# A stack of four graph layers on one core: two of four low parts moved from GpSimd to VectorE, and the hand-written order of all four engines changed

## The chip, the cores and the metric

The kernel runs on one core of a Trainium2 chip. The metric is the device time in microseconds (us) of one execution. The kernel before takes 1517.57 us, the median of 3 runs (1515.54 to 1517.81).

## What is computed

128 graphs of 128 nodes with 256 features pass through four layers. Each layer normalises its input over the features, applies ReLU, works on the result and adds it back. Cut to what matters (matrices per graph, `H` is 1 where the adjacency is not 0):

```python
# layer 1: hypergraph convolutions; Dn, Be are inverse degrees
h  = relu(Dn * (H @ (Be * (H.T @ (x @ W1.T)))) + b1)      # 512 features
h  = layer_norm(h, gamma, beta)
y  = Dn * (H @ (Be * (H.T @ (h @ W2.T)))) + b2 + x
# layer 2: attention with leaky ReLU, masked at 0.5, softmax over the nodes, ELU
h  = elu(softmax(where(adj > 0.5, leaky(Wh1 + Wh2.T), NEG_INF), axis=1) @ (x @ W))
# layer 3: diffusion, T = A * exp(leaky(...)), rows normalised
h  = relu(x @ Wk0 + bk0 + (T @ x) @ Wk1 + bk1 + (T @ (T @ x)) @ Wk2 + bk2)
# layer 4: one weight per node from masked scores, softmax over the nodes
h  = softmax(sum((q @ k.T) / 8 * adj, -1), axis=nodes) * (x @ Wv.T)
```

## The kernel before

**Tiling.** The graphs are taken in 32 groups of four (`G = 4`). A tile is [128 nodes, 4 graphs, features]. The products with a weight matrix run in a split form: an operand is written as a high part in the type fp32r plus a low part, the rest that the high part leaves, and TensorE adds three passes, high times high, high times low and low times high (`split_product`, L321 for the first two passes and L325 for the last one). Products without a split run in plain fp32 (`product`, L306), transposes too (`transposes`, L434). The high part of an activation is a copy by ScalarE out of PSUM; the low part is a subtraction by VectorE or GpSimd.

**Stages.** A round works on five groups at once: `next` (group i+1: counts, degrees, norm of the input), `front` (group i: layer 1 and the attention of layer 2), `mid` (group i-1: the ELU and layer 3), `late` (group i-2: layer 4) and `tail` (group i-3: the softmax over nodes and the output). Rounds 0 to 3 and 31 to 34 are written out with what they have; rounds 4 to 30 are one loop (`rounds`, `steady=True`).

**Order.** Nothing but the text sets the order: each engine has a function `body(r)` that calls its blocks one after the other, and each block first waits on semaphores (`wait_ge`). An engine takes its blocks in that order and no other, so a block that waits holds back everything behind it on its engine. PSUM has eight banks, and many waits are for a bank to be read out.

**The blocks around the change.** On TensorE `front_w1(r, 0..3)` makes the hidden layer (512 features x 512 nodes in four parts), `mid_h2` transposes `h` of layer 3, which VectorE's `mid_ln2` wrote, and `front_w2(r, g)` multiplies the hidden layer with W2. The first wait of `front_w2(r, 0)` is for PSUM bank 3, in which ScalarE's `tail_exp` reads the row of the tail group. `mid_p1`, `mid_p2` and `mid_p0` are the three products of layer 3, all out of the transposes. `tail_row` and `tail_turn` turn the tail group's weights there and back. ScalarE's `copy_u` (L744) writes each part of the hidden layer twice, `hT` in fp32 and `hT_hi` in fp32r, and `copy_h2T` (L754) writes the high part of the transposes. The low parts of the hidden layer are `front_lo(r, 0..3)` on GpSimd (L961), an fp32 subtraction of two SBUF tiles, 128x512; in round 0 alone VectorE makes the third and the fourth (`first_low`, L1116). TensorE's last pass of `front_w2` waits until all four are there:

```python
wait(pe, S["wex_ready"], r.tail(G))        # front_w2, g = 0 and 1
pe.wait_ge(S["hT_hi"], r.front(G))
split_product(..., 0, (S["hT_lo"], r.front(G))).then_inc(S["zr_ready"], 1)
```

GpSimd also adds the hidden layer up for its variance (`add_h` L975, `add_squares` L966, `join_h` L979, `join_squares` L971; TensorE's `front_sums` needs both results), computes every `rsqrt` as a power of -0.5 (L954 and L956), and does the elementwise sums `add_res0`, `mask_edges`, `add_xb`, `add_x4`, `add_bias` and `add_x3`. VectorE's `mid_low` (L1120) makes the low part of the transposes out of PSUM, `mid_columns` (L1301) waits for `rs2_ready`, which GpSimd's `rsqrt(2, ...)` gives. In round 0 GpSimd's `wide_lows` (L1042) makes the low parts of the weights of layers 3 and 4.

**Queues.** SyncE issues all loads and stores; no engine of the four issues a DMA. In every round it loads the adjacency and the input of the next group, stores the output and copies one adjacency tile.

## Time and profile before

| what | us |
|---|---|
| median of 3 runs | 1517.57 |
| the profiled execution, its own time | 1514.74 |
| the span of its instructions | 1512.9 |
| TensorE matmuls busy | 1461.8 (97%) |
| TensorE weight loads busy | 1321.6 (87%) |
| VectorE busy | 1230.0 (81%) |
| GpSimd busy | 1067.9 (71%) |
| ScalarE busy | 945.4 (62%) |

The granted TensorE clock is 0.99 over the span. The profile was taken from an execution of its own, so its durations are held against its own time, 1514.74 us. In the rows PE is TensorE, DVE VectorE, ACT ScalarE, POOL GpSimd; L is the line of the kernel. Matmuls are pipelined and their ends are modelled, so that a row of TensorE that looks full can hold short waits; the starts show them.

### The profile page before, as it was taken

How to read it: one execution, taken by the hardware profiler on the slowest of the kernel's cores; microseconds unless marked ns; L12 is line 12 of the kernel's file. 1: busy time of each engine (PE TensorE's matmuls, PEld its weight loads, DVE VectorE, ACT ScalarE, POOL GpSimd, SP SyncE). 2: the span in 40 equal slices, each digit the busy share in tenths (PEclk: the TensorE clock that was granted, in tenths of full speed). 3: DMA queues.
4: the chain of work that ended last, by engine and by line, in shares of the span. 5: the costliest groups of instructions: out<-in, count | busy, mean ns of one | idle time of the engine just before them, and what ended most of it. 6: DMA issues, size and time to landing. Idle time of an engine off the chain costs nothing.

```text
span 1512.9 us, 35521 instructions
## 1 busy us (share of the span) xinstructions
PE 1461.8 (97%) x9944; PEld 1321.6 (87%) x9944; DVE 1230.0 (81%) x4491; ACT 945.4 (62%) x2122; POOL 1067.9 (71%) x1070
## 2 busy tenths in 40 slices
PE   7889999999999999999999999999999999999975
PEld 5779998989998988998988998988998988998964
DVE  6779888889888889888889888889888889888773
ACT  4556666766666766666766666766566766566744
POOL 5666787676787676787676787676787676787724
PEclk9999999999999999999999999999999999999997
DMA  3011011111011111011111011111011111011001
GB/s 126 22 36 36 16 50 35 49 49 49 16 46 35 49 49 49 21 42 35 49 49 49 21 42 35 49 49 49 21 42 35 49 49 49 22 41 35 28 29 50
DMA packets 75373, 62.05 MB, mean 41 GB/s; under 512 B 3013, under 2 KB 70985, under 8 KB 75338
## 3 DMA queue, kind: packets, MB, share of 16 engines
q1 hardware_dynamic: 75338, 61.63, 12.5%
q8 instruction: 16, 0.26, 0.1%
q14 instruction: 19, 0.16, 0.0%
HBM read 36.45 MB, written 16.78 MB: 35 GB/s over the span
## 4 chain that ended last, share of the span: by engine, by line
PE 69%; DVE 18%; issue 8%; ACT 2%; POOL 1%; DVEq 1%; DMA 0%; POOLq 0%; ACTq 0%; SPq 0%
PE ps L321 29%; PE ps L306 18%; PE ps L325 15%; PE ps L434 5%; DVE stats L1207 3%; PE ps L372 2%; DVE x L1295 2%; DVE h L1225 2%; DVE q L1374 2%; DVE wh L1402 2%; DVE el L1288 2%; DVE yT_lo L1116 1%; DVE pT L1380 1%; ACT ps L812 1%; DVE qmax L1386 1%
## 5 line engine op out<-in xcount | busy, mean ns | idle before, releaser
L722 ACT ACTIVATE p<-ps,rs 128x256 f32<-128x256 f32 x384 | 164.2, 472 | 275.4 <-PE ps L325 192.9
L1009 POOL TENSOR_TENSOR x3n<-p,x 128x512 f32<-128x512 f32 x64 | 80.9, 1285 | 257.0 <-ACT p L802 257.0
L961 POOL TENSOR_TENSOR hT_lo<-hT,hT_hi 128x512 fp32r<-128x512 f32 x126 | 162.9, 1295 | 65.3 <-ACT hT_hi L744 59.2
L956 POOL TENSOR_TENSOR rs<-var_e,neg_half 128x4 f32<-128x4 f32 x160 | 165.0, 1031 | 23.7
L321 PE MATMUL ps<-wl_hi,h2T_hi 128*128 128x256 f32 (+1 forms) x768 | 168.9, 301 | 0.0
L325 PE MATMUL ps<-wl_hi,h2T_lo 128*128 128x256 f32 (+1 forms) x768 | 154.5, 283 | 0.0
L321 PE MATMUL ps<-wl_lo,h2T_hi 128*128 128x256 f32 (+1 forms) x768 | 154.4, 282 | 0.0
L434 PE MATMUL ps<-ident,h 128*128 128x128 f32 x768 | 131.9, 283 | 11.9 <-DVE h L1225 5.9
L722 ACT ACTIVATE vqk<-ps,rs 128x384 f32<-128x384 f32 x128 | 74.1, 579 | 106.8 <-POOL rs L956 60.8
L306 PE MATMUL ps<-p,alT 128*128 128x256 f32 (+1 forms) x512 | 127.1, 380 | 0.8 <-DVE z L1346 0.8
L434 PEld LDWEIGHTS ps<-ident,h 128*128 128x128 f32 x768 | 90.4, 145 | 41.7 <-DVE h L1225 19.6
L321 PEld LDWEIGHTS ps<-wl_hi,h2T_hi 128*128 128x128 f32 x768 | 120.9, 190 | 2.4 <-issue 0.2
L321 PEld LDWEIGHTS ps<-wl_lo,h2T_hi 128*128 128x128 f32 x768 | 118.4, 189 | 0.0
L325 PEld LDWEIGHTS ps<-wl_hi,h2T_lo 128*128 128x128 f32 x768 | 118.0, 189 | 0.0
L1225 DVE TENSOR_SCALAR_CACHE_REDUCE h<-x,mv 128x256 f32<-128x256 f32 x256 | 113.6, 463 | 2.3
L1207 DVE BATCH_NORM_STATS2 stats<-x 128x6 f32<-128x256 f32 x256 | 108.6, 424 | 4.5
L306 PEld LDWEIGHTS ps<-p,alT 128*128 128x128 f32 x512 | 89.7, 189 | 14.3 <-issue 1.6
L744 ACT ACTIVATE hT<-ps,cols_sb 128x512 f32<-128x512 f32 x128 | 87.8, 686 | 9.9 <-PE ps L325 8.0
L1301 DVE TENSOR_TENSOR sij<-ps,rs 128x8 f32<-128x8 f32 x32 | 5.3, 167 | 108.4 <-POOL rs L956 105.0
L1020 POOL TENSOR_TENSOR p<-p,bk 128x512 f32<-128x512 f32 x64 | 82.7, 1292 | 13.1 <-ACT p L722 12.2
L744 ACT ACTIVATE hT_hi<-ps,cols_sb 128x512 fp32r<-128x512 f32 x128 | 87.6, 684 | 3.5
L321 PE MATMUL ps<-w_hi,hT_hi 128*128 128x256 f32 x512 | 88.3, 295 | 1.1
(176 smaller groups left out, 4565.2 us busy)
## 6 DMA issues: line engine op xcount, KB each, us to landing
x_in<-in_x SPq DMA_DIRECT2D x32, 512.0 KB, 4.5
out_x<-x SPq DMA_DIRECT2D x32, 512.0 KB, 2.9
adj_f<-in_adjT SPq DMA_DIRECT2D x32, 256.0 KB, 3.6
adj_m<-in_adjT SPq DMA_DIRECT2D x32, 256.0 KB, 2.8
adj_l<-adj_m SPq DMA_DIRECT2D x32, 256.0 KB, 2.3
vqk<-in_l_wk SPq DMA_DIRECT2D x3, 256.0 KB, 4.7
x<-in_w2T SPq DMA_DIRECT2D x1, 512.0 KB, 6.6
x<-in_w1T SPq DMA_DIRECT2D x1, 512.0 KB, 7.5
```

Source lines behind the costliest of these rows:

```text
L306: last = pe.matmul(dst, lhsT(c), rhs(c), start=(c == 0), stop=(c == chunks - 1))
L321: pe.matmul(dst, lhsT(a, c), rhs(b, c), start=(a == b == c == 0), stop=False)
L325: last = pe.matmul(dst, lhsT(1 - late, c), rhs(late, c), start=False, stop=(c == chunks - 1))
L434: last = pe.transpose(ps[:, banks[b], ((g % 2) * KC + c) * P:((g % 2) * KC + c + 1) * P], h[:, g, c * P:(c + 1) * P], ident[:])
L722: return act.activation(dst, src, ACT.Copy, scale=scale)
L744: act.activation(dst[:, hc, :], ps[:, U_BANKS[hc], :], ACT.Relu, bias=cols_sb[:, 0, hc:hc + 1]).then_inc(S[ready], 1)
L956: pool.tensor_tensor(rs[:, layer, :], var_e[:, layer, :], neg_half[:], ALU.pow).then_inc(done, G)
L961: pool.tensor_tensor(hTs[1][:, hc, :], hT[:, hc, :], hTs[0][:, hc, :], ALU.subtract).then_inc(S["hT_lo"], 1)
L1009: pool.tensor_tensor(x3n[:, s], p0[:, s], x2[:, s], ALU.add).then_inc(S["x3_ready"], 2)
L1020: pool.tensor_tensor(p0[:, s, :], p0[:, s, :], bk[:].rearrange("p (a d) -> p a d", a=1) .broadcast_to((P, 2, D)), ALU.add).then_inc(S["p0b ...
L1207: dve.bn_stats(stats[:, layer, g, :], src[:, g, :]).then_inc(st, 1)
L1225: dve.tensor_scalar(dst[:, g, :], src[:, g, :], mv[:, layer, g, 0:1], None, ALU.subtract, ALU.add, accum_out=unread[:, layer, g:g + 1]).th ...
```

## The change

GpSimd no longer makes the low parts 2 and 3 of the hidden layer; VectorE does, in every round (`hidden_low`, the old `first_low` under a new name), and on all four engines blocks stand in another order. In `gnn_stack` nothing else differs: no instruction is added or left out but that two subtractions change their engine, and no buffer, bank or wait is changed. The diff, with twelve leading blanks of each line left out:

```diff
@@ -606,47 +606,49 @@
     if r.has_front:
         front_w1(r, 0)
         front_w1(r, 1)
+        front_w1(r, 2)
+        front_w1(r, 3)
     if r.has_tail:
         tail_row(r)
-    if r.has_front:
-        front_w1(r, 2)
-        front_w1(r, 3)
     if r.has_mid:
         mid_h2(r, 0)
         mid_h2(r, 1)
+        mid_p1(r, 0)
+        mid_p1(r, 1)
     if not r.steady and r.i == 0:
         second_rows(r)
         first_weights(r)
     if r.has_front:
         front_w2(r, 0)
     if r.has_mid:
-        mid_p1(r, 0)
+        mid_p2(r, 0)
     if r.has_tail:
         tail_turn(r)
     if r.has_mid:
-        mid_p2(r, 0)
         mid_p2(r, 1)
         mid_p2(r, 2)
         mid_p2(r, 3)
     if r.has_front:
         front_w2(r, 1)
     if r.has_mid:
-        mid_p1(r, 1)
         mid_b2(r)
-    if r.has_front:
-        front_w2(r, 2)
-    if r.has_mid:
         mid_p1(r, 2)
+    if r.has_front:
+        front_sums(r, 0)
+    if r.has_mid:
         mid_p1(r, 3)
+    if r.has_front:
+        front_sums(r, 1)
     if r.has_late:
         late_h3(r, 0)
     if r.has_front:
-        front_sums(r, 0)
-        front_sums(r, 1)
         front_sums(r, 2)
-        front_sums(r, 3)
     if r.has_late:
         late_h3(r, 1)
+    if r.has_front:
+        front_sums(r, 3)
+        front_w2(r, 2)
+    if r.has_late:
         late_vqk(r, 0)
     if r.has_front:
         front_w2(r, 3)
@@ -655,31 +657,32 @@
         mid_ap(r, 1)
         mid_ap(r, 2)
         mid_ap(r, 3)
+    if r.has_late:
+        late_vqk(r, 1)
     if r.has_front:
         front_c2(r, 0)
         front_c2(r, 1)
+    if r.has_mid:
+        mid_az(r, 0)
+    if r.has_front:
         front_c2(r, 2)
-    if r.has_late:
-        late_vqk(r, 1)
+    if r.has_mid:
+        mid_az(r, 1)
     if r.has_front:
         front_c2(r, 3)
     if r.has_mid:
-        mid_az(r, 0)
-        mid_az(r, 1)
         mid_p0(r, 0)
         mid_p0(r, 1)
     if r.has_next:
         next_s(r, 0)
+        next_s(r, 1)
     if r.has_mid:
         mid_p0(r, 2)
-    if r.has_next:
-        next_s(r, 1)
+        mid_az(r, 2)
+    if r.has_front:
+        front_h1(r, 0)
     if r.has_mid:
         mid_p0(r, 3)
-    if r.has_front:
-        front_h1(r, 0)
-    if r.has_mid:
-        mid_az(r, 2)
         mid_az(r, 3)
     if r.has_front:
         front_h1(r, 1)
@@ -839,35 +842,36 @@
         copy_u(r, 1)
         copy_u(r, 2)
         copy_u(r, 3)
+    if r.has_mid:
+        copy_h2T(r, 0)
+    if r.has_front:
+        square(r, 0)
     if r.has_tail:
         tail_exp(r)
     if r.has_mid:
-        copy_h2T(r, 0)
         copy_h2T(r, 1)
     if r.has_front:
-        square(r, 0)
         square(r, 1)
     if r.has_tail:
         weigh(r, 0)
+    if r.has_mid:
+        copy_p1(r, 0)
     if not r.steady and r.i == 0:
         wide_hi()
     if r.has_mid:
         copy_p2(r, 0)
         copy_p2(r, 1)
-        copy_p1(r, 0)
         exp_edges(r, 0)
         exp_edges(r, 1)
         copy_p1(r, 1)
+        copy_p2(r, 2)
     if r.has_late:
         copy_h3T(r, 0)
-    if r.has_mid:
-        copy_p2(r, 2)
-    if r.has_late:
         copy_h3T(r, 1)
+    if r.has_mid:
+        copy_p2(r, 3)
     if r.has_tail:
         weigh(r, 1)
-    if r.has_mid:
-        copy_p2(r, 3)
     if r.has_late:
         copy_vqk(r, 0, 6)
     if r.has_mid:
@@ -876,6 +880,7 @@
         copy_s(r, 0)
     if r.has_late:
         copy_vqk(r, 1, 7)
+        keep_x3(r)
     if r.has_next:
         copy_s(r, 1)
     if r.has_front:
@@ -886,9 +891,6 @@
         copy_h1T(r, 1)
     if r.has_next:
         norm_x(r, 0)
-    if r.has_late:
-        keep_x3(r)
-    if r.has_next:
         norm_x(r, 1)
     if r.has_late:
         copy_vqk(r, 2, 2)
@@ -896,10 +898,10 @@
         softmax(r, 0)
     if r.has_late:
         copy_vqk(r, 3, 3)
+    if r.has_front:
+        softmax(r, 1)
     if r.has_next:
         copy_yT(r, 0)
-    if r.has_front:
-        softmax(r, 1)
     if r.has_mid:
         relu_p0(r)
     if r.has_next:
@@ -1054,48 +1056,48 @@
 def body(r):
     if r.has_front:
         front_lo(r, 0)
+        add_h(r, 0)
         front_lo(r, 1)
-    if r.has_front and (r.steady or r.i > 0):
-        front_lo(r, 2)
-        front_lo(r, 3)
-    if r.has_front:
-        add_h(r, 0)
+    if r.has_mid:
+        rsqrt(2, mv[:, 2, :, 1], S["ag2"], r.mid(G), S["var2"], S["rs2_ready"])
+    if r.has_front:
+        add_h(r, 1)
         add_squares(r, 0)
-        add_h(r, 1)
-    if r.has_mid:
-        rsqrt(2, mv[:, 2, :, 1], S["ag2"], r.mid(G), S["var2"], S["rs2_ready"])
-    if r.has_front:
         add_squares(r, 1)
         join_h(r)
         join_squares(r)
         add_res0(r, 0)
-        add_res0(r, 1)
     if r.has_mid:
         mask_edges(r)
-    if r.has_front:
-        rsqrt(4, hmean[:, 1, :], S["hvar_ready"], r.front(G), S["vare_h"], S["rsh_ready"])
     if not r.steady and r.i == 0:
         wide_lows()
     if r.has_late:
         rsqrt(3, mv[:, 3, :, 1], S["ag3"], r.late(G), S["var3"], S["rs3_ready"])
+    if r.has_front:
+        rsqrt(4, hmean[:, 1, :], S["hvar_ready"], r.front(G), S["vare_h"], S["rsh_ready"])
+    if r.has_next:
+        rsqrt(0, mv[:, 0, :, 1], S["ag0"], r.next(G), S["var0"], S["rs0_ready"])
+    if r.has_tail:
+        add_x4(r, 0)
+    if r.has_front:
+        add_res0(r, 1)
     if r.has_next:
         add_xb(r, 0)
     if r.has_tail:
-        add_x4(r, 0)
-    if r.has_next:
-        rsqrt(0, mv[:, 0, :, 1], S["ag0"], r.next(G), S["var0"], S["rs0_ready"])
+        add_x4(r, 1)
+    if r.has_mid:
+        add_bias(r, 0)
+    if r.has_front:
+        rsqrt(1, mv[:, 1, :, 1], S["ag1"], r.front(G), S["var1"], S["rs1_ready"])
+    if r.has_mid:
+        add_bias(r, 1)
+    if r.has_next:
         shift_x(r)
-        add_xb(r, 1)
-    if r.has_tail:
-        add_x4(r, 1)
-    if r.has_mid:
-        add_bias(r, 0)
-    if r.has_front:
-        rsqrt(1, mv[:, 1, :, 1], S["ag1"], r.front(G), S["var1"], S["rs1_ready"])
-    if r.has_mid:
-        add_bias(r, 1)
+    if r.has_mid:
         add_x3(r, 0)
         add_x3(r, 1)
+    if r.has_next:
+        add_xb(r, 1)
 
 def first(r):
     rsqrt(0, mv[:, 0, :, 1], S["ag0"], r.next(G), S["var0"], S["rs0_ready"])
@@ -1191,7 +1193,7 @@
     dve.wait_ge(S["cols_ready"], 4)
     dve.memset(c0[:, 4:5], 0.0).then_inc(S["cols_ready"], 1)
 
-def first_low(r, hc):
+def hidden_low(r, hc):
     dve.wait_ge(S["hT_hi"], r.front(hc + 1))
     dve.wait_ge(S["hT_ready"], r.front(hc + 1))
     low(hTs, (slice(None), hc), hT[:, hc, :]).then_inc(S["hT_lo"], 1)
@@ -1457,8 +1459,6 @@
 
 def body(r):
     if not r.steady and r.i == 0:
-        first_low(r, 2)
-        first_low(r, 3)
         first_dots()
     if r.has_mid:
         elu_low(r, 0)
@@ -1472,40 +1472,42 @@
     if r.has_mid:
         elu_high(r, 0)
         elu_high(r, 1)
+        mid_ln2(r)
     if r.has_tail:
         tail_max(r)
     if r.has_mid:
-        mid_ln2(r)
+        mid_low(r, 0)
+    if r.has_front:
+        hidden_low(r, 2)
+        hidden_low(r, 3)
+    if r.has_tail:
+        tail_norm(r)
+    if r.has_mid:
+        mid_low(r, 1)
     if r.has_next:
         next_count(r)
     if r.has_tail:
-        tail_norm(r)
-    if r.has_mid:
-        mid_low(r, 0)
-    if r.has_next:
-        next_inverse(r)
-    if r.has_mid:
-        mid_low(r, 1)
-    if r.has_tail:
         tail_out(r)
+    if r.has_next:
+        next_moments(r)
     if r.has_mid:
         mid_columns(r)
     if r.has_late:
         late_ln3(r)
-    if r.has_next:
-        next_moments(r)
     if r.has_mid:
         mid_edges(r)
+    if r.has_next:
+        next_inverse(r)
     if r.has_late:
         late_low(r, 0)
     if not r.steady and r.i == 0:
         second_dots()
     if r.has_front:
         front_variance(r)
+    if r.has_next:
+        next_binc(r)
     if r.has_late:
         late_low(r, 1)
-    if r.has_next:
-        next_binc(r)
     if r.has_front:
         front_z(r, 0)
         front_z(r, 1)
@@ -1523,9 +1525,11 @@
         degree_masked(r)
     if r.has_front:
         front_low(r, 0)
+    if r.has_mid:
+        mid_vb(r, 0)
+    if r.has_front:
         front_low(r, 1)
     if r.has_mid:
-        mid_vb(r, 0)
         mid_vb(r, 1)
     if r.has_front:
         front_columns(r)
@@ -1536,18 +1540,17 @@
         front_logits(r, 1)
         front_leaky(r, 0)
         front_max(r, 0)
+    if r.has_next:
+        next_penalty(r)
+    if r.has_front:
         front_leaky(r, 1)
-    if r.has_next:
-        next_penalty(r)
-    if r.has_front:
         front_max(r, 1)
         front_inverse(r, 0)
         front_values(r, 0)
-    if r.has_next:
-        y_low(r.next(2), 0)
-    if r.has_front:
         front_inverse(r, 1)
         front_values(r, 1)
+    if r.has_next:
+        y_low(r.next(2), 0)
 
 def first(r):
     next_count(r)
```

## Rows read from the trace of the kernel before

**Rows 1.** The page, busy time of the engines.

```profile
PE 1461.8 (97%) x9944; PEld 1321.6 (87%) x9944; DVE 1230.0 (81%) x4491; ACT 945.4 (62%) x2122; POOL 1067.9 (71%) x1070
```

**Rows 2.** Waits in 190 to 1412 us (who waited: us in total, times, longest).

```profile
PEld ps L321 <- ACT wex L749: 7.5, 27, 0.3
DVE sij L1301 <- POOL rs L956: 89.0, 27, 3.3
```

**Rows 3.** The chain that ended last, 725.7 to 741 us (start, us, what).

```profile
739.45 0.48 DVE h L1225 x3
```

**Rows 4.** Timeline of TensorE in a steady round (start, us, what, [idle before]).

```profile
739.24 1.80 PE L434 MATMUL ps<-ident,h 128*128 128x128 f32 x8
741.08 0.74 PE L321 MATMUL ps<-w_hi,hT_hi 128*128 128x256 f32 x4
741.66 0.62 PE L321 MATMUL ps<-w_lo,hT_hi 128*128 128x256 f32 x4
742.19 0.74 PE L325 MATMUL ps<-w_hi,hT_lo 128*128 128x256 f32 x4
742.77 0.40 PE L321 MATMUL ps<-wl_hi,h2T_hi 128*128 128x256 f32 x2
```

**Rows 5.** Timeline of VectorE in the same round.

```profile
735.41 1.28 DVE L1295 SCALAR_TENSOR_TENSOR x<-ps,el 128x512 f32<-128x512 f32 x2
736.75 0.28 DVE L1417 TENSOR_REDUCE wsm<-ps 4x1 f32<-4x128 f32 x1
736.96 0.41 DVE L1207 BATCH_NORM_STATS2 stats<-x 128x6 f32<-128x256 f32 x1
...
740.47 0.28 DVE L1234 TENSOR_SCALAR_CACHE_REDUCE inc_T<-adj_f 128x128 f32<-128x128 f32 x1
...
741.36 0.14 DVE L1439 RECIPROCAL wsm<-wsm 4x1 f32<-4x1 f32 x1
...
741.91 0.67 DVE L1120 SCALAR_TENSOR_TENSOR h2T_lo<-ps,h2T_hi 128x512 fp32r<-128x512 f32 x1
```

**Rows 6.** Timeline of ScalarE in the same round.

```profile
738.07 0.69 ACT L744 ACTIVATE hT<-ps,cols_sb 128x512 f32<-128x512 f32 x1 [0.22 <-PE ps L325]
...
740.02 0.68 ACT L744 ACTIVATE hT<-ps,cols_sb 128x512 f32<-128x512 f32 x1
...
740.93 1.05 ACT L754 ACTIVATE h2T_hi<-ps 128x512 fp32r<-128x512 f32 x2
```

**Rows 7.** Timeline of GpSimd in the same round.

```profile
736.56 2.66 POOL L961 TENSOR_TENSOR hT_lo<-hT,hT_hi 128x512 fp32r<-128x512 f32 x2 [1.39 <-ACT hT_hi L744]
...
745.83 0.26 POOL L954 TENSOR_SCALAR var_e<-mv 128x4 f32<-128x4 f32 x1
746.24 1.03 POOL L956 TENSOR_TENSOR rs<-var_e,neg_half 128x4 f32<-128x4 f32 x1
```

**Rows 8.** Timeline of the start, VectorE and GpSimd: two-tile subtractions that overlap.

```profile
20.03 1.22 DVE L1149 TENSOR_TENSOR w_lo<-x,w_hi 128x1024 fp32r<-128x1024 f32 x1
20.48 1.93 POOL L961 TENSOR_TENSOR hT_lo<-hT,hT_hi 128x512 fp32r<-128x512 f32 x1 [1.53 <-ACT hT_hi L744]
23.61 1.72 POOL L975 TENSOR_TENSOR hsq<-hT 128x512 f32<-128x512 f32 x1
24.62 1.26 DVE L1116 TENSOR_TENSOR hT_lo<-hT,hT_hi 128x512 fp32r<-128x512 f32 x1 [0.42 <-ACT hT L744]
```

**Rows 9.** Timeline of the start: GpSimd's power and VectorE's scalings inside it.

```profile
8.34 1.10 POOL L956 TENSOR_TENSOR rs<-var_e,neg_half 128x4 f32<-128x4 f32 x1
9.04 0.88 DVE L1132 TENSOR_SCALAR x<-x,cols_sb 128x256 f32<-128x256 f32 x3 [0.22 <-DMA x<-in_w2T]
```

**Rows 10.** Timelines of rounds 0 and 1, GpSimd and TensorE.

```profile
36.34 0.25 POOL L954 TENSOR_SCALAR var_e<-hmean 128x4 f32<-128x4 f32 x1 [1.88 <-DVE hmean L1338]
37.76 3.46 POOL L1042 TENSOR_TENSOR wl_lo<-vqk,wl_hi 128x512 fp32r<-128x512 f32 x3
...
80.57 0.67 PE L306 MATMUL ps<-p,alT 128*128 128x257 f32 x2 [0.77 <-DVE z L1346]
```

18 lines of the change are left out of this document (9 added, 9 removed).

## The prediction, made before the changed kernel had run

> **What bounds the kernel now.** I read the page first: TensorE's matmuls are busy 97% of the span, VectorE 81%, GpSimd 71% [rows 1]. Then the waits of the loop's stretch: what stands there 27 times stands there once a round, so a round is 1222 / 27 = 45.26 us [rows 2]. Four rounds written out, 27 in the loop and four to drain make up the rest.
>
> A TensorE that is 97% busy would leave only the number of matmuls to save, and the change saves none. So I read the chain that ended last and the timelines. In every round the chain leaves TensorE after the transposes of the degrees (about 726 us in the round shown), runs through VectorE, the softmax, the ELU and the norm of layer 3 up to the last `h` [rows 3], and comes back to TensorE when the eight transposes of `h` can end: eight of them take 1.80 us there [rows 4], where they would take about 0.9 at TensorE's pace of 0.11 us each, which I take from the four matmuls of 128x256 that start within 0.45 to 0.58 us [rows 4]. So a round is one loop of two pieces: about 15 us of VectorE, and 30 us of TensorE in which it has no real slack. What shortens the round is a wait inside the TensorE piece or an instruction inside the VectorE piece. What ends on GpSimd or ScalarE counts only where one of the two waits for it.
>
> In the TensorE piece I see two waits right behind the transposes. `front_w2(r, 0)` waits for ScalarE's `tail_exp`: 7.5 us in 27 rounds, 0.28 us each [rows 2]. Its last pass then waits for GpSimd's fourth low part: the starts 741.66, 742.19 and 742.77 are 0.53 and 0.58 us apart where four such matmuls at full pace take 0.46 (741.66 is itself a pass at full pace), so 0.07 of wait and 0.12 of restart, 0.19 in all [rows 4]. GpSimd is late in another place too: VectorE's `mid_columns` waits 3.3 us a round for `rs2` [rows 2], but the products `mid_p2` that it also needs end only shortly before, so this wait costs nearly nothing.
>
> **The change, part by part, per steady round.**
>
> *TensorE after the transposes.* `mid_p1(0)` and `mid_p1(1)` now come first, then `front_w2(0)`. The wait for `tail_exp` goes: the two products stand before it (0.7 us each: three passes at about 0.24 from the start at 742.77 on), minus 0.28. The wait for the fourth low part goes as well, minus 0.19. New is that `mid_p1(0)` has no cover between the transposes and their copy. The first half of the transposes is ready near 740.0; ScalarE is free after its last `hT` copy, which now comes as before or a little earlier, 740.0 to 740.1 + the copy of 0.57 [rows 6], so the high part is there at 740.7, as TensorE arrives: no wait. VectorE's `mid_low(0)` starts when the copy ends and its end is 0.67 later [rows 5], 741.45, where TensorE wants it at about 741.3 (two high passes and 0.11 for the start): 0.1 to 0.2 of wait and a restart of 0.11, plus 0.3.
>
> *VectorE, the two low parts.* No instruction of a steady round is a subtraction of two SBUF tiles by VectorE. A VectorE operation of 128x512 that reads PSUM takes 0.68 and starts its follower 0.60 later (two `elu_high` in 1.28) [rows 5]; alone I take the same, 2 x 0.60 = 1.2 us. They stand between `mid_low(0)` and `tail_norm`, in the 3.3 us in which VectorE waits for `rs2` [rows 2], so they cost nothing by themselves; but `mid_low(1)` stands behind them and `mid_p2(0)` waits for it. Times: `mid_low(0)` 740.8, the two low parts 741.4 and 742.0, `tail_norm` 742.6 to 743.15 (0.55 from its first start to the next block [rows 5]), `mid_low(1)` up to 743.8. TensorE has two `mid_p1` and one `front_w2` (1.5) behind the wait above and comes to `mid_p2(0)` at about 743.9. Cost 0 to 0.1, and I take 0.05.
>
> *VectorE's piece of the loop.* `tail_max` leaves it: between the end of `elu_high` at 736.69 and the norm's first start at 736.96 lie 0.27 us [rows 5]; without it a gap of 0.06, as in front of 736.75, is left: minus 0.2. `next_penalty` now stands ahead of the second `front_leaky` instead of between it and its `front_max`, so a gap of such a size opens: plus 0.07. Sum minus 0.13.
>
> *GpSimd.* Two subtractions of about 1.3 [rows 7] go, 2.6 us a round. `rs2` comes some 4 us earlier, and `mask_edges`, `rs4` and `join_squares` earlier too. Nothing in the steady loop waits for these now but `mid_columns`, so I count 0. `shift_x` and the second `add_xb` move to the end: `shift_x` ends about 1 us before VectorE's part for the attention needs ScalarE again, and `norm_x` fits in ScalarE's idle time there. 0.
>
> *The other moves* (`mid_az` between `front_c2`, `front_sums` between `mid_p1` and `late_h3`, `next_moments` into VectorE's idle time, `mid_vb(0)` between the `front_low`, `softmax(1)` ahead of a copy) keep the matmuls of TensorE's piece the same set. `front_att` ends 0.4 us earlier, but this lies beside VectorE's piece: 0. `mid_az(0)` waits for `mid_z1(0)`, which needs all four `mid_ap`; `late_vqk(1)` and two `front_c2` cover it. No queue of SyncE is passed.
>
> Sum of a steady round: -0.28 - 0.19 + 0.3 + 0.05 - 0.13 = -0.25 us; the bounds are -0.5 (no new wait) and +0.1 (both new waits twice as long). Over 28 rounds: -7 us, bounds -14 and +3.
>
> *The start.* In round 0 `wide_lows` now stands ahead of `rsqrt(4)`. Three of its four operations take 3.46, the fourth has 768 columns instead of 512, about 1.7: 5.2 us; against this GpSimd had waited 1.88 for the variance [rows 10], and one `add_res0` (1.3) moves behind: z comes 2.0 us later, plus 2.0. In round 1 TensorE waits 0.77 for z [rows 10] and more for GpSimd before it, since the whole round hangs on GpSimd there; 2.6 us less of it give about -1.2, round 2 about -0.5. Sum +0.3. In the drain `tail_max` stands in the norm's way once: -0.3.
>
> Sum: 1514.74 - 7 + 0 = 1507.7 for the profiled execution, minus 7 (0.5%). The median shown is 2.8 above that execution, so 1517.57 - 7 = 1510.5.
>
> **The lock between VectorE and GpSimd.** In the start two-tile operations of both overlap. GpSimd's subtraction at 20.48 began inside VectorE's of 20.03 to 21.25 and took 1.93 instead of 1.3; VectorE's at 24.62 began inside GpSimd's addition of 23.61 to 25.33 and took 1.26 instead of 0.68 [rows 8]. So the later one stands still until the earlier one is done, or nearly. Where do the new subtractions fall? GpSimd in the steady round: third `hT` copied at 738.3 (ScalarE, 738.07 before, some 0.4 earlier now) [rows 6], `add_h(0)`, `front_lo(1)` of 1.25 each, 0.4 for the add of epsilon, the power of 1.03 [rows 7]: the power runs 741.2 to 742.25, then `add_h(1)`. The subtractions run 741.4 to 742.6: beside the power. That power took 1.10 at 8.34 to 9.44, and VectorE's three scalings started inside it at their own pace, 0.88 for three [rows 9]; so a power does not hold VectorE, and I count 0. Only GpSimd's `add_h(1)` is put off by 0.4, and `join_squares` still ends 0.5 us before `front_sums`.
> The Trainium skill (SBUF — State Buffer, "SBUF: two separate sides") says that the shared pair of ports is an exclusive lock which the operation that starts first holds for the whole instruction, for a VectorE operation with two SBUF inputs against a GpSimd one that reads SBUF. The trace agrees on the elementwise ones [rows 8]; on the power no row here has a two-input VectorE operation. By that rule the time would be that of the third rival.
>
> **The rivals.**
> 1. *The new waits eat it.* If `mid_p1(0)` waits 0.4 for copy and low part and `mid_p2(0)` 0.2, the round stays within 0.1 of 45.26: 1514 to 1520. For it speaks that every margin above is under 0.2 us. Chance 0.19.
> 2. *The second low part meets `add_h(1)`.* The margin is 0.25 us (742.0 against 742.25). If VectorE is later by that, it stands still for 1.25, `mid_low(1)` ends at 745.2, and `mid_p2(0)` waits 1.3 more: a round of -0.25 + 1.3 = +1.05, over 28 rounds +29: 1547; met in a part of the rounds, or with part of the wait covered, 1521 to 1547. It decides once VectorE comes to the second low part over 0.25 us later than above. Against it: both engines start from the same ScalarE copies. Chance 0.15.
> 3. *The power holds the lock.* The first low part, started 0.2 after the power, stands still 0.85, and the second then falls behind `add_h(1)`: 0.85 + 1.25 = 2.1 a round minus 0.25 and 0.05 of margin, +1.8, over 28 rounds +50: 1567. The scalings in [rows 9] speak against it. Chance 0.06.
> 4. *The forecast*, a round of 44.75 to 45.15: 1503 to 1514. Chance 0.6.
>
> **How the numbers follow.** A measurement of this kernel can tell about 0.2% (3 us) from no change. Faster by more: 0.6, the forecast. Within: 0.18, most of the first rival. Slower: 0.22, rivals 2 and 3 and the rest of the first. The range takes the forecast with its bounds and the first rival and part of the second: 1502 to 1526; outside are the full rivals 2 and 3 and a small chance below.
>
> **What would show it.** In the profile after: no row of `PEld ps L321 <- ACT wex`; TensorE's `ps<-wl_hi,h2T_hi` directly behind the transposes, its `h2T_lo` pass 0.1 to 0.3 late; the steady round 45.0; VectorE's `hT_lo` rows at about 0.68, beside GpSimd's power, and not at 1.2 or more; VectorE's wait for `rs` gone; GpSimd's `wl_lo` ahead of `rs` in round 0 and z 2 us later. Wrong I would be if the `hT_lo` rows are stretched, if `mid_p2(0)` waits for `h2T_lo` by more than 0.3, or if a steady round is 45.2 or longer.

## The result, and the profile after

The changed kernel took 1531.71 us (median of 4 runs, 1531.37 to 1533.54) against 1517.69 (4 runs, 1515.54 to 1519.71) of the kernel before: the ratio is 1.010, with a 95% interval of 1.0087 to 1.0113. It is slower by 1%, where I had forecast 1510.5 and a range up to 1526. The profiled execution took 1531.81 with a span of 1530.0, 17.1 us longer than the span of before. The medians are 14.0 apart: the profiled execution of before, 1514.74, lies 3 us under its median, that of after on it, so some 3 of the 17 belong to the two executions and not to the kernels.

Where the 17 us of the profiles lie can be read from the start of the first `w1` matmul of each round. Each column is the time between two such starts (rounds 4 to 31: the mean of 27), in us:

| | round 0 | rounds 1 to 3 | a round, 4 to 31 | last stretch |
|---|---|---|---|---|
| before | 39.50 | 133.14 | 45.27 | 100.54 |
| after | 42.96 | 133.34 | 45.70 | 102.49 |
| loss | +3.5 | +0.2 | +0.43 x 27 = +11.6 | +1.9 |

The last stretch begins with round 31, which still has its front part. If that round lost 0.43 as the others did, the drain itself lost 1.5.

The page, busy time of the engines, against [rows 1]:

```profile
PE 1471.3 (96%) x9944; PEld 1330.9 (87%) x9944; DVE 1279.2 (84%) x4553; ACT 938.1 (61%) x2122; POOL 1006.8 (66%) x1008
```

The move is plainly there: VectorE does 62 instructions and 49 us more, GpSimd 62 fewer and 61 us less.

The waits of the steady rounds, 193 to 1427 us, against [rows 2] (who waited: us in total, times, longest):

```profile
PEld ps L325 <- DVE yT_lo L1118: 9.2, 27, 0.3
DVE h2T_lo L1122 <- ACT h2T_hi L757: 8.5, 27, 0.3
...
DVE sij L1303 <- PE ps L325: 6.3, 26, 0.2
...
PEld ps L325 <- DVE h2T_lo L1122: 5.3, 27, 0.2
```

The two waits that I read before are gone: nobody waits for `wex` any more, and `sij` no longer waits for GpSimd's power. In their place TensorE's weight loads wait for two low parts, that of y (0.34 us a round) and that of h2 (0.20). The wait for y lies ahead of the transposes of h2, in a stretch in which the round waits for VectorE anyway.

Timelines of a steady round, against [rows 4 to 7] (start, us, what, idle before). TensorE:

```profile
748.22 1.94 PE L434 MATMUL ps<-ident,h 128*128 128x128 f32 x8
750.21 0.47 PE L321 MATMUL ps<-wl_hi,h2T_hi 128*128 128x256 f32 x2
750.51 0.40 PE L321 MATMUL ps<-wl_lo,h2T_hi 128*128 128x256 f32 x2
750.91 0.51 PE L325 MATMUL ps<-wl_hi,h2T_lo 128*128 128x256 f32 x2
...
751.97 0.64 PE L321 MATMUL ps<-w_hi,hT_hi 128*128 128x256 f32 x4
```

ScalarE, VectorE and GpSimd at the same place:

```profile
748.89 0.68 ACT L747 ACTIVATE hT<-ps,cols_sb 128x512 f32<-128x512 f32 x1
749.46 0.60 ACT L757 ACTIVATE h2T_hi<-ps 128x512 fp32r<-128x512 f32 x1
...
749.58 0.27 DVE L1419 TENSOR_REDUCE wsm<-ps 4x1 f32<-4x128 f32 x1
750.16 0.69 DVE L1122 SCALAR_TENSOR_TENSOR h2T_lo<-ps,h2T_hi 128x512 fp32r<-128x512 f32 x1 [0.31 <-ACT h2T_hi L757]
750.77 1.28 DVE L1118 TENSOR_TENSOR hT_lo<-hT,hT_hi 128x512 fp32r<-128x512 f32 x2
...
750.76 1.59 POOL L958 TENSOR_TENSOR rs<-var_e,neg_half 128x4 f32<-128x4 f32 x1
752.33 1.29 POOL L977 TENSOR_TENSOR hsq<-hT 128x512 f32<-128x512 f32 x1
```

Three things stand in these rows. TensorE comes to its first product behind the transposes 1.99 us after their start; before it was 1.84 us [rows 4], so a wait still ends there, and it now ends with ScalarE's copy of h2 (749.46 + 0.60 = 750.06). The third pass begins at 750.91, 0.40 behind the second instead of the 0.24 of a pass at pace, because VectorE's `h2T_lo` ends at 750.85. And the two new subtractions take 1.28 together, at their own pace, beside GpSimd's power; it is the power that is stretched, to 1.58 or 1.59 instead of 1.03 [rows 7], in 24 of the 27 steady rounds.

### The profile page after: what moved, and what is told of

Same layout as the page of the kernel before. It is cut to its first block, busy times and chain, and to the rows that moved or that the text cites. A ratio compares the mean times of both kernels' runs of the same rounds, so it can differ in the third digit from the quotient of the medians.

```text
span 1530.0 us, 35520 instructions
## 1 busy us (share of the span) xinstructions
PE 1471.3 (96%) x9944; PEld 1330.9 (87%) x9944; DVE 1279.2 (84%) x4553; ACT 938.1 (61%) x2122; POOL 1006.8 (66%) x1008
## 4 chain that ended last, share of the span: by engine, by line
PE 80%; DVE 11%; issue 5%; ACT 2%; DMA 0%; DVEq 0%; POOL 0%; POOLq 0%; ACTq 0%; SPq 0%
PE ps L321 31%; PE ps L306 25%; PE ps L325 15%; PE ps L434 5%; DVE stats L1209 3%; PE ps L372 3%; DVE h L1227 2%; DVE x L1297 2%; DVE el L1290 1%; ACT ps L815 1%; DVE mv L1213 1%; PE ps L603 0%; DMA x_in<-in_x 0%; DVE yT_lo L1118 0%; DVE q L1376 0%
## 5 line engine op out<-in xcount | busy, mean ns | idle before, releaser
L958 POOL TENSOR_TENSOR rs<-var_e,neg_half 128x4 f32<-128x4 f32 x160 | 180.0, 1125 | 23.7
L321 PE MATMUL ps<-wl_hi,h2T_hi 128*128 128x256 f32 (+1 forms) x768 | 178.9, 314 | 2.6 <-ACT h2T_hi L757 1.0
L325 PE MATMUL ps<-wl_hi,h2T_lo 128*128 128x256 f32 (+1 forms) x768 | 158.3, 288 | 0.0
L321 PE MATMUL ps<-wl_lo,h2T_hi 128*128 128x256 f32 (+1 forms) x768 | 155.1, 283 | 0.0
L434 PE MATMUL ps<-ident,h 128*128 128x128 f32 x768 | 135.1, 285 | 16.3 <-DVE h L1227 5.8
L306 PE MATMUL ps<-p,alT 128*128 128x256 f32 (+1 forms) x512 | 136.9, 379 | 0.3 <-DVE p L1328 0.3
L321 PEld LDWEIGHTS ps<-wl_hi,h2T_hi 128*128 128x128 f32 x768 | 119.8, 191 | 11.6 <-issue 9.2
L321 PEld LDWEIGHTS ps<-wl_lo,h2T_hi 128*128 128x128 f32 x768 | 119.3, 190 | 0.0
L725 ACT ACTIVATE x<-vqk,wcol 128x256 f32<-128x256 f32 x128 | 58.0, 505 | 66.6 <-DVE wcol L1424 66.6
L963 POOL TENSOR_TENSOR hT_lo<-hT,hT_hi 128x512 fp32r<-128x512 f32 x64 | 83.6, 1306 | 20.3 <-ACT hT_hi L747 20.3
L998 POOL TENSOR_TENSOR alT<-zb,adj_m 128x512 f32<-128x512 f32 x32 | 41.1, 1286 | 83.2 <-DVE zb L1316 83.2
L977 POOL TENSOR_TENSOR hsq<-hT 128x512 f32<-128x512 f32 x64 | 83.6, 1306 | 18.4 <-ACT hT L747 18.4
L794 ACT ACTIVATE h<-x_in,nmr,rs 128x256 f32<-128x256 f32 x128 | 66.5, 590 | 46.8 <-POOL nmr L992 46.8
```

Source lines behind the costliest of these rows:

```text
L306: last = pe.matmul(dst, lhsT(c), rhs(c), start=(c == 0), stop=(c == chunks - 1))
L321: pe.matmul(dst, lhsT(a, c), rhs(b, c), start=(a == b == c == 0), stop=False)
L325: last = pe.matmul(dst, lhsT(1 - late, c), rhs(late, c), start=False, stop=(c == chunks - 1))
L434: last = pe.transpose(ps[:, banks[b], ((g % 2) * KC + c) * P:((g % 2) * KC + c + 1) * P], h[:, g, c * P:(c + 1) * P], ident[:])
L725: return act.activation(dst, src, ACT.Copy, scale=scale)
L958: pool.tensor_tensor(rs[:, layer, :], var_e[:, layer, :], neg_half[:], ALU.pow).then_inc(done, G)
```

## The experiments

All kernels are the one before or after with blocks of one or more engines put elsewhere; none leaves work out. The ratios are to the kernel before, run on the same chip. The last three columns are of one profiled execution of each kernel, "a round" being the mean of rounds 4 to 30.

| | median us | ratio to before, 95% | round 0 | a round | last stretch |
|---|---|---|---|---|---|
| e1 after, `wide_lows` later | 1533.44 | 1.0104 (1.0086 to 1.0122) | 42.12 | 45.67 | 103.02 |
| e2 after, h2 part as before | 1523.73 | 1.0041 (1.0026 to 1.0056) | 42.67 | 45.43 | 102.21 |
| e3 after, h3 part as before | 1528.87 | 1.0071 (1.0058 to 1.0085) | 42.98 | 45.51 | 103.82 |
| e4 before, the move alone | 1512.77 | 0.9971 (0.9960 to 0.9982) | 38.77 | 45.23 | 100.11 |
| e5 after, e2 + e3 + GpSimd as before | 1514.50 | 0.9986 (0.9977 to 0.9994) | 39.05 | 45.29 | 103.27 |
| e6 after, GpSimd as before | 1560.34 | 1.0284 (1.0271 to 1.0297) | 39.56 | 46.75 | 103.96 |
| e7 after, the move undone | 1573.43 | 1.0360 (1.0326 to 1.0393) | 42.64 | 47.20 | 103.44 |
| e8 e4, `tail_exp` earlier | 1514.28 | 0.9982 (0.9973 to 0.9991) | 40.72 | 45.22 | 101.57 |
| e9 before, `tail_exp` earlier | 1519.08 | 1.0018 (1.0009 to 1.0027) | 40.01 | 45.39 | 100.85 |
| e10 e4, one low part moved | 1518.99 | 1.0014 (1.0004 to 1.0024) | 40.56 | 45.34 | 100.70 |
| e11 e8, one low part moved | 1514.15 | 0.9977 (0.9964 to 0.9990) | 40.56 | 45.14 | 101.35 |
| e12 e11 in the steady rounds only | 1508.59 | 0.9939 (0.9926 to 0.9953) | 38.74 | 45.00 | 102.48 |

The columns for round 0 and the last stretch hold something besides the order: TensorE's granted clock. In both it falls to 0.50, the 1.2 GHz level, for some us at a time, and not for equally long in every profile. What that costs can be read in e7, where the same steady round stands with and without it (stretches of e7: from and to, length, busy time of the engines, then the granted clock):

```profile
389.60:436.00 46.40, 45.29 (x312) 41.17 (x311) 38.16 (x140) 29.20 (x66) 33.12 (x34) 1.00 0.12 39
436.00:485.60 49.60, 48.55 (x312) 44.41 (x311) 38.30 (x140) 29.20 (x66) 33.09 (x34) 0.93 0.11 37
456.50:462.50 6.00, 6.00 (x26) 6.00 (x26) 3.77 (x15) 2.23 (x5) 5.04 (x8) 0.50 0.00 0
```

The round with 6.8 us at the lower level is 3.2 us longer, rounds with 3.4 us at it are 1.6 longer. In the steady rounds of all other kernels the granted clock is 1.00, so their column "a round" is free of this.

### e4: the move alone

```diff
 (before, GpSimd)
-                    front_lo(r, 2)
-                    front_lo(r, 3)
 (before, VectorE; first_low taken out of the start of round 0)
                     mid_ln2(r)
+                    first_low(r, 2)
+                    first_low(r, 3)
                     tail_norm(r)
                     mid_low(r, 0)
                     mid_low(r, 1)
+                    next_count(r)
+                    next_inverse(r)
```

> Kernel before, with the move of the low parts alone: the third and fourth made by VectorE right behind the second layer norm, GpSimd's taken out, all other blocks in the order of before. Theory 1 (the move itself costs nothing; what after lost is the order): VectorE's low parts take about 0.68 us each, since GpSimd is idle there, W2 no longer waits for the fourth low part (0.19 us a round), the steady round is 45.05 to 45.25 against 45.27, total 1511 to 1517. Rival (the move is the loss: VectorE's longer piece or the lock between the two engines): the low parts are stretched to 1.2 us or more or VectorE's tail becomes late, the round is 45.5 or more and the total 1524 or more.

Measured: 1512.77, the round 45.23, and VectorE's low parts at their own pace (VectorE by line and form, 190 to 1405 us: busy us, mean ns | idle before):

```profile
L1112 DVE TENSOR_TENSOR hT_lo<-hT,hT_hi 128x512 fp32r<-128x512 f32 x54 | 34.8, 686 | 0.0
```

The move is not quite alone: VectorE's `next_count` and `next_inverse` went behind both low parts of h2, so that these come earlier.

Theory 1 holds in its signs: the move is a gain of 0.3%, nothing is stretched, and TensorE's W2 products take 0.22 us a round less (sum over their starts in the trace). Only 0.04 of it reached the round: the turn took 0.10 more, since VectorE's `tail_norm` is now behind two low parts, and another 0.1 went inside VectorE's attention block (see the last section). The span is 4.1 us shorter: 0.8 by an earlier first `w1`, 0.7 in round 0, 0.9 in the next three, 1.1 in the 27 steady rounds, 0.4 in the last stretch. So the loss of the changed kernel is in its order, or in the move as that order places it, and not in the move by itself.

### e2 and e3: two parts of the order, put back one at a time

```diff
 (after, TensorE; e2)
                     front_w1(r, 1)
+                    tail_row(r)
                     front_w1(r, 2)
 ...
                     mid_h2(r, 1)
+                    front_w2(r, 0)
                     mid_p1(r, 0)
                     mid_p1(r, 1)
 (after, VectorE; e2)
+                    tail_max(r)
                     mid_ln2(r)
-                    tail_max(r)
-                    mid_low(r, 0)
                     hidden_low(r, 2)
                     hidden_low(r, 3)
                     tail_norm(r)
+                    mid_low(r, 0)
 (after, ScalarE; e2: tail_exp ahead of copy_h2T(r, 0); GpSimd: add_h(r, 0) behind front_lo(r, 1))
```

```diff
 (after, TensorE; e3)
                     mid_b2(r)
-                    mid_p1(r, 2), front_sums(r, 0), mid_p1(r, 3), front_sums(r, 1)
-                    late_h3(r, 0), front_sums(r, 2), late_h3(r, 1), front_sums(r, 3)
-                    front_w2(r, 2)
+                    front_w2(r, 2), mid_p1(r, 2), mid_p1(r, 3), late_h3(r, 0)
+                    front_sums(r, 0) to front_sums(r, 3), late_h3(r, 1)
```

> Kernel after, with the blocks around copy_h2T(0) put back: W2's first piece ahead of the p1 and gate pieces, ScalarE's tail_exp ahead of copy_h2T(0), VectorE's tail_max ahead of mid_ln2, VectorE's low part of h2 one place later, GpSimd's add_h(0) behind the first fourth's low part. Theory 1: in after, the piece that reads h2 is put into TensorE's order before ScalarE's and VectorE's copies are ready; its wait for the low part (0.27 us a round with the restart) goes, the steady round falls from 45.69 to about 45.43, 28 times that is 7 us, total near 1524. Rival (the wait only moves, since something else of W2 or the softmax is then late): a new wait of 0.2 us or more on TensorE behind the w1 pieces and 45.6 or more.

> Kernel after, with TensorE's pieces b2, W2 of the third fourth, the last two p1 pieces, the h transposes and the sums in the order of before. Theory 1: of the 0.42 us a round that after loses, 0.2 is the wait of the last h transpose for ScalarE's copy of p1, which stands behind 8 exponentials that wait for b2, and some 0.1 are the extra restarts of p1 between pieces of another kind; both go, the round falls to about 45.42, the total to about 1523. Rival (the loss is in the h2 part alone, and this order is neutral): 45.6 to 45.7 and a total within 3 us of after.

Measured: e2 took the round from 45.70 to 45.43 and the total to 1523.73, the numbers of its theory. The wait that the theory named is only a part of it. From VectorE's last statistics of the norm to TensorE's first product behind the transposes it is 2.44 us in after and 2.25 in e2 (means of the steady rounds), so the first product comes 0.19 earlier; behind it the p1 products (with those of `mid_p0`, which have the same form) take 0.17 less, the p2 products 0.06 less and W2's 0.10 more; `tail_max`, back in VectorE's piece, gives 0.08 of it back. W2 waiting for `tail_exp` starts earlier than p1 waiting for the copy of h2. e3 took it to 45.51, two thirds of what was expected, and the total to 1528.87: it gained 0.19 in each steady round, and lost 0.9 in round 1 and 1.3 in the last stretch. That 1.3 goes with the clock, not with the order: the last stretch has a granted clock of 0.87 against 0.89 in after, 3.5 us more at the lower level, and its 470 matmuls are busy for 78.3 us against 77.0. What e3 removes can be seen in the timeline of ScalarE and TensorE in after:

```profile
760.22 0.63 ACT L782 ACTIVATE ps<-ps,sjc 128x128 f32<-128x128 f32 x2
760.72 1.26 ACT L725 ACTIVATE p<-ps,rs 128x256 f32<-128x256 f32 x3
...
761.18 0.50 PE L306 MATMUL ps<-ones,hsq 128*128 128x1 f32 x4
761.74 0.65 PE L434 MATMUL ps<-ident,h 128*128 128x128 f32 x4
```

Four such matmuls of one column take 0.37 elsewhere in the round from their start to the next block (760.35 to 760.71), so the transposes could have begun near 761.55; they wait 0.2 for ScalarE's copies of `p1`, which stand behind eight exponentials.

In e2 VectorE's first low part of the hidden layer starts 0.10 us ahead of GpSimd's add of epsilon, and the other engine is held (GpSimd; the third row is of VectorE):

```profile
746.05 0.69 POOL L957 TENSOR_SCALAR var_e<-mv 128x4 f32<-128x4 f32 x1
746.89 1.24 POOL L959 TENSOR_TENSOR rs<-var_e,neg_half 128x4 f32<-128x4 f32 x1
...
745.95 1.29 DVE L1119 TENSOR_TENSOR hT_lo<-hT,hT_hi 128x512 fp32r<-128x512 f32 x2
```

An operation of 0.25 takes 0.69 and the power, which began inside the second low part, 1.24 instead of 1.03; the low parts keep their 0.69. This costs nothing here, since nobody waits for that power.

### e1 and e6: GpSimd's order

```diff
 (after, GpSimd; e1)
-                if not r.steady and r.i == 0:
-                    wide_lows()
                     rsqrt(3, ...)
                     rsqrt(4, ...)
+                if not r.steady and r.i == 0:
+                    wide_lows()
 (after, GpSimd; e6: all blocks in the order of before, without front_lo(r, 2) and front_lo(r, 3))
```

> Kernel after, with the start's wide_lows on GpSimd put back behind the power of the fourth group (as before). After lost 3.4 us in the start against before: z ended its wait at 41.2 instead of 37.8 us, while VectorE's tiny second_dots operations (128x4, 128x1) took 1.1 to 1.8 us each beside GpSimd's wide_lows. Theory 1 (the two engines hold each other up when wide_lows runs beside VectorE's two-input operations): these operations fall back to under 0.3 us each, z's start comes near 38 us, the first w1 of round 1 near 57.0 us instead of 60.4, the total near 1528. Rival (the time went by the order alone, VectorE has more to do in the start whatever GpSimd does): round 1 begins at 59 us or later and the total is 1530 or more. The steady round stays at 45.7 us under both.

VectorE in the start of after, in the stretch where it makes columns for the second weights, and GpSimd beside it:

```profile
33.09 0.44 DVE L1183 CAST wl_hi<-att_cols 128x4 fp32r<-128x4 f32 x1
33.45 1.22 DVE L1184 CAST wl_hi<-att_cols 128x4 fp32r<-128x4 f32 x1
34.58 1.22 DVE L1186 TENSOR_TENSOR c<-c 128x1 f32<-128x1 f32 x1
35.84 1.13 DVE L1188 TENSOR_TENSOR wl_lo<-att_cols,wl_hi 128x4 fp32r<-128x4 f32 x1
36.88 1.84 DVE L1190 TENSOR_TENSOR wl_lo<-att_cols,wl_hi 128x4 fp32r<-128x4 f32 x1
...
33.47 3.48 POOL L1044 TENSOR_TENSOR wl_lo<-vqk,wl_hi 128x512 fp32r<-128x512 f32 x3
36.90 1.80 POOL L1044 TENSOR_TENSOR wl_lo<-x3n,wl_hi 128x768 fp32r<-128x768 f32 x1
```

Four operations of one or four columns take 1.1 to 1.8 us each: each stands still beside one of GpSimd's four subtractions. In e1 the same four, and what came of it:

```profile
34.60 0.16 DVE L1184 CAST wl_hi<-att_cols 128x4 fp32r<-128x4 f32 x1
34.67 0.15 DVE L1186 TENSOR_TENSOR c<-c 128x1 f32<-128x1 f32 x1
34.85 0.16 DVE L1188 TENSOR_TENSOR wl_lo<-att_cols,wl_hi 128x4 fp32r<-128x4 f32 x1
34.93 0.15 DVE L1190 TENSOR_TENSOR wl_lo<-att_cols,wl_hi 128x4 fp32r<-128x4 f32 x1
...
45.92 0.69 DVE L1358 TENSOR_TENSOR x<-ps,res 128x512 f32<-128x512 f32 x1 [4.09 <-POOL res L1017]
```

The mechanism is shown: 0.15 us each. But the expected 3.4 us did not come. The second half of x waited 4.09 us for GpSimd's second residual, which in after's order is behind `wide_lows`; round 0 fell by 0.8 only, and the total did not move. My expectation had looked at z and not at what is queued behind `wide_lows` on GpSimd. e6 puts the residual ahead as well:

> Kernel after with GpSimd's whole order as before, without the two low parts: wide_lows behind both residuals and the power of the fourth group. e1 showed the six small VectorE operations fall back to 0.15 us each and z start 3.3 us earlier, but the second half of x then waited 4.1 us for GpSimd's second residual, which stood behind wide_lows. Theory 1 (two faults of one placement: it holds VectorE up where it is, and it holds the residual up where e1 put it): with the residual ahead too, the first w1 of round 1 comes 39.5 to 40.0 us behind that of round 0 (after: 42.96, e1: 42.12), the steady round stays at 45.7, total 1527.5 to 1529. Rival (round 0 is lost to something else in after's order): 42 us or more and no gain in the total.

Round 0 fell to 39.56, as theory 1 had it. The steady round did not stay: it went to 46.75, and the kernel to 1560.34. The reason stands in one row (VectorE by line and form, 190 to 1405 us), and in the timelines of a round, GpSimd and VectorE:

```profile
L1114 DVE TENSOR_TENSOR hT_lo<-hT,hT_hi 128x512 fp32r<-128x512 f32 x52 | 62.1, 1237 | 0.0
```

```profile
762.68 1.46 POOL L968 TENSOR_TENSOR hsq<-hsq 128x512 f32<-128x512 f32 x1 [1.49 <-ACT hsq L737]
764.10 1.73 POOL L977 TENSOR_TENSOR hsq<-hT 128x512 f32<-128x512 f32 x1
...
762.30 2.39 DVE L1114 TENSOR_TENSOR hT_lo<-hT,hT_hi 128x512 fp32r<-128x512 f32 x2
```

In before's order of GpSimd, its addition of squares comes just as VectorE makes the low parts. The first low part (762.30) runs through, the second starts inside the addition and takes 1.8 us instead of 0.68. That is the mechanism of my second rival, met by another addition, and its price is 1.05 us a round against after; W2's products alone, whose last pass waits for the low part, take 1.07 more, summed over their starts. So in the changed kernel GpSimd's new order, to which I gave the cost 0 and no purpose, is what keeps the lock from the moved low parts. It isn't needed for that everywhere: e4 and e5 have GpSimd's blocks in the order of before, other places for VectorE's, and low parts of 0.686.

The Trainium skill (SBUF — State Buffer, "SBUF: two separate sides") says that whichever of a VectorE operation with two SBUF inputs and a GpSimd one that reads SBUF starts first has the shared ports for its whole instruction. e6 and e2 agree for elementwise operations, and so do the lengths in after's start; who came first there is too close to tell (VectorE's held cast is recorded at 33.45, the subtraction at 33.47). For the power the trace of after differs. In the round shown above power and low part start 0.01 apart, and the power is held. In 3 of the 27 rounds the power is recorded 0.02 ahead, and is not (GpSimd, then VectorE):

```profile
887.78 1.04 POOL L958 TENSOR_TENSOR rs<-var_e,neg_half 128x4 f32<-128x4 f32 x1
887.80 1.32 DVE L1118 TENSOR_TENSOR hT_lo<-hT,hT_hi 128x512 fp32r<-128x512 f32 x2
```

Here the power keeps its 1.04, and the two low parts inside it take 0.72 and 0.68 (their single records; the row shows both merged). A power that isn't held costs VectorE 0.04 us, and not its own length.

### e7: the order alone

```diff
 (after, GpSimd)
                     front_lo(r, 0)
-                    add_h(r, 0)
                     front_lo(r, 1)
+                    front_lo(r, 2)        # from round 1 on
+                    front_lo(r, 3)        # from round 1 on
+                    add_h(r, 0)
 (after, VectorE: hidden_low(r, 2) and (r, 3) in round 0 only)
```

> Kernel after with its order kept and the move undone: the third and fourth low part back on GpSimd in every round but the first, ahead of its add_h, as before. This is the order alone. Theory 1 (the order makes the loss, and the move does not): the steady round stays between 45.6 and 45.8 us and the total within 3 us of after, 1529 to 1534; W2 reads the low parts 1.5 us later than in before, so they are not waited for. Rival (the loss is VectorE's extra 1.3 us in its tail): the h2 low part is ready earlier, its wait of 0.27 us a round goes, the round falls to 45.4 or less and the total to 1524 or less.

Both theories missed: 1573.43, 47.20 a round. In that mean are 8 of the 27 rounds in which the granted clock fell to 0.50 for 3.4 or 6.8 us (the rows above; in the round shown TensorE had been busy for 0.97 of 1.70 us shortly before, at 452.5). The other 19 rounds, at full clock, take 46.42. With 2.6 us more on GpSimd in front of them, its sums end late, and TensorE, which in after's order takes `front_sums` between the p1 products, waits for them (waits, 190 to 1405 us):

```profile
PEld ps L306 <- issue: 24.8, 26, 1.0
...
PE ps L306 <- issue: 19.9, 26, 0.8
```

The profile names no releaser; that these are the waits for the sums is read from their place, in front of the first `ps<-ones,hsq` matmul of a round; the block ahead of that place takes 0.9 us a round more than in after. The order needs the move, then: without it the order costs 1.15 us a round at full clock and 0.8 more by the falls of the clock, with it 0.43.

### e5: the orders put back together

```diff
 (after: the edits of e2 and e3 on TensorE, VectorE and ScalarE, that of e6 on GpSimd)
```

> Kernel after with three parts of its order put back together: the h2 part (as in e2), the h3 part (as in e3), and GpSimd's whole order as before, without the two low parts. ScalarE's and VectorE's other blocks and TensorE's later pieces stay as in after. Theory 1 (the losses are separate waits and add up): 0.30 and 0.17 us a round go, the steady round is 45.2 to 45.25, the start is that of before (first w1 of round 1 about 39.5 us behind that of round 0), total 1511 to 1515. Rival (the two losses are one, behind the same wait, and what remains of the order costs something): 45.35 us a round or more, total 1517 or more.

Measured 45.29 a round, between the theory's 45.25 and the rival's 45.35, and 1514.50, inside the theory's total. The two gains of e2 and e3 (0.27 and 0.19) add up to 0.46, and 0.40 came: they are nearly separate. The profiled execution took 1518.08, the longest of its 11 and 3.6 over their median. In its last stretch, 103.27, TensorE's 470 matmuls are busy for 77.7 us against 75.6 in before, with a granted clock of 0.88 against 0.89, so most of what that stretch grew by is not the order.

### e8 to e11: taking the wait for `wex` another way

```diff
 (e4 for e8, before for e9; ScalarE)
                     copy_u(r, 2)
+                    tail_exp(r)
                     copy_u(r, 3)
-                    tail_exp(r)
 (e8 only, VectorE: tail_norm(r) behind mid_low(r, 0))
 (e10 = e4, e11 = e8, each with: GpSimd makes the third low part; add_h(r, 0) behind add_squares(r, 0), add_h(r, 1) behind rsqrt(2, ...))
```

> The best kernel so far (e4, the move alone) with two more blocks moved: ScalarE's tail_exp ahead of copy_u of the last fourth instead of behind it, and VectorE's tail_norm behind the first low part of h2. W2 now waits 0.28 us a round for wex, the exponentials that tail_exp makes, and these wait only for their place on ScalarE. Theory (this was the wait the change aimed at; it can be taken without touching TensorE's order): the wait for wex goes, 0.2 to 0.28 us a round, the steady round is 44.95 to 45.05 against 45.21 in e4, total 1505 to 1508. Rival (the copy behind it becomes late by the 0.5 us that tail_exp takes, and with it the fourth high and low part): a new wait in W2 for hT_hi or hT_lo of 0.2 us or more, 45.15 us or more a round.

> Kernel before with one block moved: ScalarE's tail_exp ahead of copy_u of the last fourth. The low parts stay on GpSimd. It takes away the wait of W2 for wex (0.28 us a round) and nothing else. Theory 1 (behind this wait stands the next one: GpSimd's fourth low part, already waited for by 0.19 us, is not ready earlier, so W2's third pass starts when it did): W2 begins 0.28 us earlier and waits for hT_lo by 0.4 us or more instead of 0.19, the steady round stays within 45.2 to 45.35 us and the total within 2 us of before. Rival (the waits are worth their size each by itself): 45.0 us a round, total near 1509.

> Kernel e4 (the move alone) with one low part moved instead of two: the third is back on GpSimd behind the second, the fourth stays on VectorE. GpSimd's add_h of the first fourth goes behind its first add_squares, and the second add_h behind the power, so that none of its adds runs beside VectorE's low part. Theory (VectorE has 0.6 us less between the second layer norm and h2's low parts, GpSimd had 2.6 us of idle time there): W2 still does not wait for hT_lo, and the turn and p2 lose the 0.1 us by which they are now longer; the steady round is 45.05 to 45.2 against 45.21, total 1508 to 1513. Rival (GpSimd's later sums now arrive late at TensorE or its power at VectorE): 45.3 us or more a round and 1515 or more.

> e8 (tail_exp ahead of the last copy_u, on top of the move alone) with the third low part back on GpSimd, GpSimd's adds placed as in e10. In e8 W2 no longer waited for wex, but p2 then waited 0.22 us for VectorE's second low part of h2, the last of five blocks that VectorE does behind the second layer norm. Theory (that chain of VectorE, with the 1.2 us of the two moved low parts in it, is what bounds e8): with one low part less on VectorE this wait goes, the steady round is 44.95 to 45.05 against 45.22, total 1505 to 1509. Rival (the next late thing is GpSimd, whose adds now end 1.3 us later): 45.2 us or more, and a wait on TensorE for the sums or on VectorE for the power.

e9 is the clearest of the study. The wait of W2 for `wex` is gone (the transposes' block takes 0.29 us less), and in its place stands (waits, 190 to 1405 us):

```profile
PEld ps L325 <- POOL hT_lo L962: 13.5, 27, 0.5
...
PE ps L325 <- POOL hT_lo L962: 8.0, 27, 0.3
```

0.5 us a round for the weights and 0.3 for the matmul behind them. W2's products take 0.37 us a round more, summed over their starts, against the 0.29 saved. Theory 1 had the mechanism; but the low part did not even stay where it was, since the last copy of ScalarE, which it reads, now stands behind `tail_exp`. The round grew by 0.12, and the total went just past the 2 us allowed. A wait removed alone made the kernel slower.

e8 lost the wait too, and got its own: p2 waits for VectorE's second low part of h2 (`PE ps L321 <- DVE h2T_lo`, 0.22 us a round), so the round is e4's. Neither its theory nor its rival had named this one. e10 misses: it was to be 45.05 to 45.20 and is 45.34, though W2's products stay short and the turn is back at 0.15; against before 0.10 are in the first `p,alT` products and 0.1 in VectorE's attention block. Its numbers are those of its rival (45.3 or more, 1515 or more), but no row of its waits shows the rival's cause, GpSimd's sums or power coming late. e11 comes to 45.14, and only a part of what was expected: `PE ps L321 <- DVE h2T_lo` falls to 1.1 us in 6 rounds, yet the turn still takes 0.37 instead of 0.15. Round 0 lost 1.8 us against e4 in both; it has a granted clock of 0.87 there against 0.91, 3.4 us more at the lower level, which at e7's price is up to 1.6 of it.

### e12: a version that beats both

e11's places in the steady rounds, e4's in the first rounds and in the drain; each moved block stands twice:

```diff
 (e4, ScalarE; the same for tail_norm, the third low part and the two add_h)
+                if r.steady and r.has_tail:
+                    tail_exp(r)
                     copy_u(r, 3)
-                if r.has_tail:
+                if not r.steady and r.has_tail:
                     tail_exp(r)
```

> e11's order in the steady rounds, e4's (the move alone) in the first rounds and in the drain. e11's steady round took 45.13 us against e4's 45.21, but its round 0 took 40.56 us from first w1 to first w1 against 38.77, and its last stretch 101.35 against 100.11. Theory (these losses hang on the blocks' order in the unsteady rounds, where GpSimd and ScalarE have other neighbours): round 0 back to 38.8, the last stretch to 100.1 to 100.4, the steady round at 45.13, the total 2 to 3 us below e4, 1509.5 to 1511.5. Rival (the losses come with the steady order, for instance by the round that follows): 1513 or more.

Measured 1508.59, ratio 0.9939: faster than the kernel before by 0.6%, than the changed one by 1.5%. Round 0 is back at 38.74. The last stretch stayed long (102.48), against the theory, although its order is e4's. It goes with the clock again (e12, then e4):

```profile
1403.20:1505.70 102.50, 77.50 (x470) 67.22 (x468) 60.30 (x203) 50.80 (x115) 45.93 (x44) 0.87 0.09 32
1408.70:1508.80 100.10, 75.14 (x470) 65.44 (x468) 60.33 (x203) 50.80 (x115) 45.93 (x44) 0.88 0.10 33
```

The same 470 matmuls are busy for 2.4 us more, all that the stretch is longer by, and e12 has 3.0 us more at the lower level in it. Whether the kernel or the single execution brings that is not shown. The total is below the theory's 1509.5 to 1511.5 all the same, because the steady round is 45.00 and not 45.13, for which the last section has a place and no cause. Of the 0.23 by which this round is shorter than e4's, about half is that tenth: e4 has it in front of `gt`, e12 has it nowhere.

## Why the prediction was wrong, point by point

**TensorE after the transposes: the step that failed.** The prediction said "ScalarE is free after its last `hT` copy, which now comes as before or a little earlier, 740.0 to 740.1 + the copy of 0.57 [rows 6], so the high part is there at 740.7, as TensorE arrives: no wait". 740.02 is the start of that last `hT` copy [rows 6], not its end. Its own 0.57 to 0.68 was left out: 740.02 + 0.57 + 0.60 for the copy of h2 is 741.2, not 740.7. The trace after shows the chain: the transposes start at 748.22, the last `hT` copy at 748.89 (0.67 later; before 0.78, so "a little earlier" was right), h2's copy at 749.46, its end at 750.06, TensorE's product at 750.21. Before, W2 began behind `tail_exp` 1.84 us after the transposes' start [rows 4]; from VectorE's last statistics to the first product, which leaves out that the transposes start a little earlier in after, it is 2.43 us before and 2.44 after (means of the steady rounds), the same. `copy_h2T(0)` had taken `tail_exp`'s place on ScalarE, and TensorE waited for the one as it had for the other. So the "minus 0.28" did not come. The prediction had ScalarE's queue before it, and took one row's start for its end.

**The other waits.** The low part of h2 was put at 0.3 with its restart, and sized rightly: 0.40 - 0.24 for the third pass and 0.11, 0.27 in the trace. The fourth low part's 0.19 went: W2's first piece takes 1.39 us after and 1.69 before, of which 0.11 is a restart that now falls on p1. `mid_p2(0)`, put at 0.05, has no row in the waits. As forecast these terms make -0.19 + 0.3 + 0.05 = +0.16; the sign of this part hung on the 0.28.

**The other moves, put at 0,** cost about 0.2. That was the second failure: I had checked that the set of matmuls is the same, and not what each new neighbour waits for. e3, which undoes these in TensorE, gives 0.19 a round. There is the wait of the last h transposes for ScalarE's copy of p1, 0.2, and perhaps 0.1 for p1 products that begin behind a block of another kind; e3 does not part the two.

**VectorE's piece** was put at -0.13 and is +0.05 (13.03 us before, 13.08 after, from TensorE's transposes of the degrees to VectorE's last statistics of the norm, means of the steady rounds). `tail_max` out of it gave -0.20 and `next_penalty` +0.09, both nearly as forecast; 0.11 more stand in front of `gt`, which no block of the change explains, and 0.05 are spread.

**The lock.** Forecast: the low parts run beside the power at 0.68. Measured: 0.68, beside the power. The row that the forecast leaned on had no VectorE operation with two SBUF inputs, but it held: no low part was held for the length of a power, the most that one lost is 0.04 us (3 rounds of after). In the other 24 rounds the power lost 0.55, which the forecast had not named; it delays GpSimd's `add_h(1)`, and nobody waits for it. Rival 2 did not happen in after: `add_h(1)` starts 0.95 us behind the second low part in the round shown (752.33 against 751.38) and 0.35 behind it in those 3 rounds, where the forecast had 0.25. That its mechanism is real e6 shows, where it costs 1.05 us a round against after (I had priced the wait at 1.3). Rival 3 did not happen either.

**The start** was put at +0.3 and is +3.7 (+3.5 in round 0, +0.2 in the next three rounds). The step was "z comes 2.0 us later"; it came 3.4 later (41.24 against 37.82), and from there to round 1 both kernels take 19.1. I had counted what `wide_lows` takes of GpSimd's time, and not whom it holds. Six small operations of VectorE take 5.7 us from first to last (33.09 to 38.80), where e1 needs 0.9 for them (34.24 to 35.16); GpSimd's add of epsilon for this variance, at 36.34 before [rows 10], starts at 39.76. The -1.2 and -0.5 expected of rounds 1 and 2 were -0.4 and +0.1.

**The drain** was put at -0.3 and is +1.5. The granted clock of the last stretch is 0.89 before and after, so it is not the clock. In part it is `mid_b2`, which waits there for a copy of ScalarE, 0.96 us where it had waited 0.26 (timeline of TensorE, after):

```profile
1486.93 0.62 PE L372 MATMUL ps<-ident,sij 128*128 128x128 f32 x4 [0.96 <-ACT p L725]
```

The cause of the rest is open.

Summed per round: 0 instead of -0.28, -0.19, 0.27 instead of 0.3, 0 instead of 0.05, 0.2 instead of 0, 0.05 instead of -0.13: +0.33, and 0.43 was measured. What is missing is not in one place: between the first product and the next transposes of the degrees the p2 products take 0.15 more a round, the products of the degrees (`binc_T,inc_T`) 0.08 more and those of layer 4 0.09 less, and no run moves one of these alone. The first rival, "the new waits eat it", had the mechanism and a size too small: it allowed 0.1 around 45.26.

## What to carry to other kernels

Take a queue's next free time from the end of its last row, and write both the start and the duration of each link down; margins of 0.2 us don't survive one duration left out. A wait that is removed can uncover the next one behind it: e9 took 0.28 us of wait away and its round grew by 0.12, so first list what is late next, and move that too (e4, then e8 and e11, then e12). And read another engine's order as part of the change even where it ends in slack: what an idle-looking engine does at that moment decides whether its neighbour stands still (e6, e1). Before a stretch that is not steady is laid to an order, its granted clock has to be compared (e3, e12), and a mean over rounds looked at round by round (e7).

## What the runs showed that I had not expected

**Small operations pay the full lock.** A VectorE operation of one column stands still for a whole GpSimd subtraction of 512 columns: 1.22 instead of 0.15. A cast, with one input, is held like a two-input operation (33.45, 1.22). Between elementwise operations the one that is held waits for the rest of the other's instruction: 1.8 against 0.68 in e6, 0.69 against 0.25 in e2. GpSimd's power is the exception: it can be held, but where it is not it takes 0.04 us from VectorE and not its length.

**The same order, 0.13 us apart.** e11 and e12 have the same blocks in the same order in every steady round, and most rounds take 45.13 and 45.00. Of the 0.13, 0.10 lies between two operations of VectorE's attention block. e11:

```profile
772.53 0.41 DVE L1378 SCALAR_TENSOR_TENSOR pT<-q 128x256 f32<-128x256 f32 x1
773.15 0.42 DVE L1384 TENSOR_REDUCE qmax<-pT 128x2 f32<-128x256 f32 x1 [0.21 <-DVE pT L1378]
```

e12:

```profile
767.95 0.42 DVE L1388 SCALAR_TENSOR_TENSOR pT<-q 128x256 f32<-128x256 f32 x1
768.47 0.42 DVE L1394 TENSOR_REDUCE qmax<-pT 128x2 f32<-128x256 f32 x1
```

The reduction starts 0.62 or 0.63 us behind its input in 26 of 27 steady rounds of e11, and 0.51 or 0.52 in all of e12. In after and e4 a tenth of the same size stands in front of `gt` instead (0.38 of wait for TensorE where before has 0.27). In these kernels it stays at one place in every steady round, and it changes place from kernel to kernel. Its cause is open: e11 and e12 differ in the code of their unsteady rounds, and no run tells what of it matters. It means that two orders of this kernel can't be told apart by less than about 0.1 us a round, 3 us in all, unless their timelines are laid side by side; some 0.1 of after's 0.43, the 0.11 in front of `gt`, looks to be of this kind.
